# One-hots of low index digits moved from VectorE to ScalarE, and a node piece's first products one slot later, in a two-layer graph network on one core

## What is computed

```python
summed = jax.ops.segment_sum(h[src], dst, num_segments=N_NODES)
return h @ W_self + (summed * deg_inv[:, None]) @ W_neigh + b
...
h = relu(sage_conv(x, ...W_self1, W_neigh1, b1))
h = sage_conv(h, ...W_self2, W_neigh2, b2)
x = layernorm(x + h)
```

## Time and profile before

| | us |
|---|---|
| median of 3 runs | 8132.46 |
| lowest and highest | 8115.67, 8134.15 |
| profiled execution | 8146.79 |
| its span | 8144.9 |

### The profile page before, as it was taken

The page is one execution under the profiler, slowest core; times in us unless marked ns, Lnnn a source line. Parts: engine busy times, 40 slices in busy tenths (PEclk is TensorE's granted clock), DMA queues, the critical chain, the costliest instruction groups (busy, mean ns, idle before and its releaser), DMA issues. The chain is left out here.

```text
span 8144.9 us, 106831 instructions
## 1 busy us (share of the span) xinstructions
PE 6048.0 (74%) x32520; PEld 3961.2 (49%) x32520; DVE 5361.4 (66%) x11308; ACT 2438.4 (30%) x2998; POOL 5785.3 (71%) x5857
## 2 busy tenths in 40 slices
PE   5678787777766788888767777777777777777776
PEld 4555555444444556555534444444444444444444
DVE  8988877676754555555366666666666666666666
ACT  2111111111111000000034444444444444444454
POOL 7777665555555777777757777777777777777776
PEclk8889988888887998899878888888888888888888
DMA  4466667666666898898744444444444444444443
GB/s 123 150 196 234 222 229 246 223 234 221 235 235 228 289 313 302 303 309 305 258 151 130 130 131 131 129 133 131 129 132 133 132 134 134 133 133 132 134 135 103
DMA packets 598851, 1523.91 MB, mean 187 GB/s; under 512 B 157137, under 2 KB 290917, under 8 KB 587014
## 3 DMA queue, kind: packets, MB, share of 16 engines
q1 hardware_dynamic: 411075, 1133.17, 41.0%
q0 software_dynamic: 187200, 383.76, 16.6%
HBM read 1374.92 MB, written 141.47 MB: 186 GB/s over the span
## 5 line engine op out<-in xcount | busy, mean ns | idle before, releaser
L1704 POOL DMA_INDIRECT messages_rows<-y_d,src_idx x3125 | 3043.2, 974 | 1003.3 <-issue 949.0
L1110 POOL DMA_INDIRECT sum_x_rows<-in_x,sum_x_edges x1525 | 1572.5, 1031 | 848.0 <-issue 427.9
L1110 POOL DMA_INDIRECT sum_z_rows<-z_d,sum_z_edges x1200 | 1168.1, 973 | 478.7 <-issue 347.6
L1782 PE MATMUL messages_p_msg<-Wm_e,messages_gated 128*128 128x128 f32 x6250 | 1002.8, 326 | 496.4 <-DVE messages_below L1907 496.1
L1782 PEld LDWEIGHTS messages_p_msg<-Wm_e,messages_gated 128*128 128x128 f32 x6250 | 926.5, 235 | 876.2 <-issue 875.1
L1897 DVE TENSOR_TENSOR messages_p_msg<-messages_p_msg,messages_rows 128x1024 f32<-128x1024 f32 x391 | 481.6, 1232 | 1207.8 <-DMA messages_rows<-y_d,src_idx 1024.8
L1212 PE MATMUL sum_x_build<-sum_x_key_hot,sum_x_low_hot 128*128 128x490 bf16 (+2 forms) x2900 | 833.5, 374 | 230.0 <-DVE sum_x_counts L1408 225.4
L1814 ACT ACTIVATE messages_parts<-messages_p_msg 128x1024 bf16<-128x1024 f32 x391 | 400.1, 1023 | 1808.7 <-DVE messages_p_msg L1897 1808.7
L1232 PE MATMUL sum_z_p_loaded<-sum_z_split,sum_z_counts 128*128 128x384 bf16 x2744 | 794.3, 347 | 160.7 <-DMA sum_z_split<-z_parts_d 156.7
L1408 DVE SCALAR_TENSOR_TENSOR sum_x_counts<-sum_x_counts,sum_x_build 128x980 f32 (+3 forms) x635 | 647.6, 1020 | 356.9 <-PE sum_x_build L1212 346.1
L1232 PE MATMUL sum_x_p_prod<-sum_x_split,sum_x_counts 128*128 128x385 bf16 x2744 | 692.2, 345 | 190.8 <-DMA sum_x_split<-x_parts_d 163.6
(11 more groups left out here) (273 smaller groups left out, 9173.7 us busy)
## 6 DMA issues: line engine op xcount, KB each, us to landing
sum_x_split<-x_parts_d SPq DMA_DIRECT2D x392, 675.5 KB
sum_z_split<-z_parts_d SPq DMA_DIRECT2D x392, 675.5 KB
messages_when<-in_edge_weight SPq DMA_DIRECT2D x391, 512.0 KB, 4.0
messages_attr<-in_span_attr SPq DMA_DIRECT2D x391, 256.0 KB
counts_d<-sum_x_counts SPq DMA_DIRECT2D x28, 3136.0 KB
sum_z_counts<-counts_d SPq DMA_DIRECT2D x56, 1568.0 KB
messages_rows<-y_d,src_idx POOLq DMA_INDIRECT x3125
sum_x_rows<-in_x,sum_x_edges POOLq DMA_INDIRECT x1525
```

The lines of the kernel that those rows point to most:

```text
L1110: nc.gpsimd.indirect_dma_start(out=rows[:, s % depth, j, :], out_offset=None, in_=table, in_offset=bass.IndirectOffsetOnAxis(ap=edges[:, b ...
L1704: nc.gpsimd.indirect_dma_start(out=rows[:, g % SPAN_DEPTH, j, :], out_offset=None, in_=d["y"], in_offset=bass.IndirectOffsetOnAxis(ap=src_ ...
L1782: last = nc.tensor.matmul(p_msg[:, j * P:(j + 1) * P], gated[:, g % SPAN_GATEDS, j * P:(j + 1) * P], t.Wm_e[:], start=True, stop=True)
```

## The change

The low-digit one-hot of five counted tiles is made on ScalarE, in both sums, by six instructions in place of VectorE's one: five Abs of 128 columns (the digit as the bias, so that each gives the distance of the column to the digit) into a new buffer `low_far`, and one Relu of 1 minus that over 640 columns into `low_hot`. ScalarE does it in the slot in which VectorE did, after the copy of the group's one-hot and before everything else. It waits for the digits (`keys_ready`), for the ring (`built`) and for its own instructions. VectorE's `keys_of` now waits until ScalarE has read the digits of two chunks ago. In sum_x, step 3 of a piece on TensorE becomes step 4, and step 4 on ScalarE step 5.

```diff
     def tensor(pe, n, s):
-        if s == 3:
+        if s == 4:
             pe.wait_ge(xT_in, n * 16 + 16)
...
     def scalar(act, n, s):
-        if s == 4:
+        if s == 5:
             act.wait_ge(hB_set, 2 if fast else 1)
...
     low_hot = sb("low_hot", [P, lows, P], BF16)
+    low_far = sb("low_far", [P, TILES, P], BF16)
...
+    low_far_ready = sem("low_far_ready")
...
-                    if first and n == 0 and step == 3:
+                    if first and n == 0 and step == 4:
                         begin.tensor_pieces(pe)
...
+            def low_tiles(u):
+                chunk, at = u // BODY, u % BODY
+                act.wait_ge(keys_ready, chunk * KEY_LINKS + 5)
+                wait_for(act, built, plan.unit_of[u - lows + TILES - 1] + 1 if u >= lows else 0)
+                wait_for(act, low_hot_ready, u // TILES)
+                for j in range(TILES):
+                    last = nc.scalar.activation(low_far[:, j, :], t.iota[:], ACT.Abs, bias=low[:, chunk % 2, at + j:at + j + 1], scale=-1.0)
+                last.then_inc(low_far_ready, 1)
+                act.wait_ge(low_far_ready, u // TILES + 1)
+                nc.scalar.activation(low_hot[:, u % lows:u % lows + TILES, :], low_far[:], ACT.Relu, bias=t.ones_col[:, 0:1], scale=-1.0
+                                     ).then_inc(low_hot_ready, 1)
...
                     nc.scalar.copy(hot16[:, s % WINDOW_HOTS], hot[:, s % WINDOW_HOTS]).then_inc(hot_halved, 1)
+                for u in tiles_of(units_at[s]):
+                    if u % TILES == 0:
+                        low_tiles(u)
                 for b, z in clears_at[s]:
...
                 dve.wait_ge(counted_in[chunk % 3], 16 * (chunk // 3 + 1))
+                wait_for(dve, low_hot_ready, (chunk - 1) * UNROLL)
...
-                if u % TILES == 0:
-                    wait_for(dve, built, plan.unit_of[u - lows + TILES - 1] + 1 if u >= lows else 0)
-                    nc.vector.tensor_tensor(
-                        low_hot[:, u % lows:u % lows + TILES, :], t.iota[:].unsqueeze(1).to_broadcast([P, TILES, P]),
-                        low[:, ring, at:at + TILES].unsqueeze(2).to_broadcast([P, TILES, P]), ALU.is_equal).then_inc(low_hot_ready, 1)
```

## The result

The changed kernel took 8083.75 us (median of 4 runs, 8075.42 to 8090.3) against 8129.35 us (8115.67 to 8134.15). The ratio is 0.9942, with an interval of 0.9925 to 0.9959: 0.58% or 47 us faster, where 100 us were forecast. The profiled execution took 8090.3 us, 56.5 us less than that of before.

The account below looks back on a forecast made before the run. It took sum_z as paced by GpSimd, and sum_x after 600 us as TensorE and VectorE waiting in turn. Terms -40 - 85 - 10 - 45 + 45 + 15 + 20 gave -100 us: 8032, 8-in-10 range 7860 to 8165.

Parts of the forecast that it names:

- Until 600 us: -40: Early sum_x: relieving VectorE gains 40 us (bounds 0 and 53), limited by GpSimd's lead.
- Products one slot later, -85 and clock -10: Sum_x pieces: the `z_rest` wait goes, partly filled by building a unit, -85 us; products at a higher clock, -10.
- Counts, -45: Sum_x after 600 us: TensorE's 92.5 us of waits for VectorE's counts shrink, -45 us (bounds 0 and -92).
- Flips, +45: 28 slots where a block's product ends: new ScalarE instructions ahead of the clears delay the copies, +45 us.
- Late one-hots, +15: Where a chunk of 25 tiles begins: ScalarE's one-hot comes 1.6 us later than VectorE's did, +15 us in all.
- Table chunks, +20: Sum_x: a faster TensorE asks for table chunks sooner and waits longer for them, +20 us (0 to +65).
- Sum_z, 0: Sum_z: GpSimd's gathers set the pace, so the change is worth between 0 and -57 us, taken as 0.
- The price of a group: ScalarE's five Abs and one Relu for five tiles: 2.4 us, with bounds 2.0 and 2.8.
- GpSimd's pace: Rival in sum_x: removed waits free both engines until GpSimd sets the pace; -250 us, 7882, chance 0.16.
- waits renamed: Rival: TensorE's waits only change name, about 8125, chance 0.12; its sign is GpSimd's wait hardly moving.
- slower through ScalarE's order: Rival at the 28 flips: a block pays 5 to 8 us, not 2.4; about 8183, chance 0.11.
- The table load at each change of function: Rival on ScalarE: Abs and Relu share no table and reload at 1.283 us; about +120, 8250, chance 0.03.

Follow-up runs that it names:

- flips_first: The changed kernel with ScalarE's low one-hots behind the clears and copies in slots that copy a product; ratio 0.9869 to the kernel before.
- tables_first: The changed kernel with ScalarE's low one-hots behind the clears and table split, still ahead of the product copies; ratio 0.9895 to the kernel before.
- one_hots_last: The changed kernel with ScalarE's order in every slot: table split, product copies, clears, low one-hots, piece steps; 7969.17 us, ratio 0.9793 to the kernel before.
- pieces_only: The kernel before with only the pieces' products one slot later, low one-hots left on VectorE; ratio 0.9909, 74 us faster.
- digits_only: The changed kernel with the piece steps put back, low one-hots still on ScalarE; ratio 1.0025 to the kernel before, 20 us slower.
- order_without_digits: The kernel before with products one slot later and product copies ahead of clears, low one-hots on VectorE; ratio 0.9878 to the kernel before.
- the two repairs: The changed kernel with early_on_vector and flips_first joined; 7995.49 us, ratio 0.9828 to the kernel before.
- early_on_vector: The changed kernel with the low one-hots of sum_x's first 300 tiles (slots 10 to 40) left on VectorE; ratio 0.9916 to the kernel before.
- copies_first: The changed kernel with early_on_vector and flips_first joined, and the clears also behind the product copies; ratio 0.9801 to the kernel before.

## Why the prediction was wrong

**The sign and the later terms held; the early path did not.** The failed step is the first term, *Until 600 us: -40*. It reckoned with VectorE, relieved, and GpSimd, at its pace, and with nothing else: ScalarE's order was priced at the flips and where chunks begin, but never in the early slots, where it holds the table split that VectorE waits for. In its place stood a loop through both engines: at slot 84, near 600 us, the kernel was 13 us late, and not 40 us early. (About 12 us of this gap are the first flips, which the forecast had in another term: flips_first reaches slot 84 at 595.2 us.) From there to the end of sum_x it gained 55 us (13 us late, then 42 early), where the forecast's later terms add up to -60. So this one step is most of the miss. With the split copies ahead (tables_first) the kernel is 38 us faster than the changed one and 29 us early at slot 84; in one_hots_last it is 39 us early. That this is just the 40 of the forecast is in part luck: GpSimd's lead at that place was 25 us, not up to 53, and shorter gathers, which the forecast did not have, gave the other 18.

**Products one slot later, -85 and clock -10.** Right in kind: alone they gave 74 us for 95. Two sizes were off against each other. The fill by a unit was overrated, as 40 of the 113 us that left `z_rest` became waits for counts; the clock was underrated: the products took 37 us less, where 30 were reckoned, and the flips took hardly any of it back (55.4 us busy before, 56.4 after), where 20 were taken off.

**Counts, -45.** The wait itself reads 92.5 and 95.9, as if the term were nothing. Taken from pieces_only it is 36 us (132.1 to 95.9): about right, and covered by what the pieces had renamed. Together with the early term, -85 for VectorE's relief stands beside the 69 us that the digits brought when they stood last, late one-hots included.

**Flips, +45.** Right: the wait grew by 51 us, and putting the one-hots behind the copies took that away and brought 60. **Late one-hots, +15**: after 600 us only 5.8 us; the 69.6 us before that were mostly the loop's. **Table chunks, +20**: +11. **Sum_z, 0**: its gathers changed little, as 63.4 for 56.8 us of waits for TensorE show; sum_z itself took 7 us less.

**The price of a group** was estimated at 2.4 us with Abs 0.38 and Relu 0.79; it measured 0.386, 0.828 and 2.34 to 2.5. By the rule of the Trainium skill (ScalarE: Activation LUTs, section Rules for kernel authors) this work belongs on VectorE. Its factor of up to about 3 is for bf16 instructions with one source; here six instructions on ScalarE (2.5 us) stand against one on VectorE with two fp32 sources (0.82 us), so that the ratio is near 3 does not test it. Digits_only is slower, as the rule would have it, but one_hots_last and order_without_digits differ by 69 us the other way: price alone did not decide here, and the place in ScalarE's list did.

**The rivals.** GpSimd's pace did not take over in this kernel: from 600 us on its wait for TensorE stayed at 410 us, and one_hots_last brought it to 289. (Until 600 us TensorE waits for gathers in one_hots_last, 34.2 us for 3.3 before.) The prediction named an unmoved wait as its sign of waits renamed; it misled. Over all of sum_x the gathers themselves took 70 us less (1572.5 and 1502.7 us busy), more than the stage became shorter, so GpSimd's wait had to grow, and did, from 418.8 to 444.0 us. Waits did change their name, in part (40 us to counts in pieces_only). The case slower through ScalarE's order had the right engine and the wrong place: 60 us at the flips, and some 40 more at the split, which it didn't name. With the digits alone it came true, by 20 us. The table load at each change of function is out: sum_x still has one load, of 1283 ns. This agrees with the Trainium skill (ScalarE: Activation LUTs, section Table sets: the hidden batching unit), by which cheap functions such as relu, copy and abs are in every set.

**What stays open.** That the two repairs together give more (93 us) than singly (21 and 60) lies inside the intervals. So does the difference of tables_first (38) and early_on_vector (21) in time. At slot 84 they are 13 us apart (564.6 and 577.1); that this is VectorE's relief in the early slots, which only tables_first keeps, was not tested by itself. The orders were tried in this one program, and the 25 us of the clears and the 22 of copies_first are hardly clear of the intervals.

## What to carry to other kernels

An engine that idles most of a stage still runs a list in order: before work is moved onto it, write down every instruction that comes to stand behind the new one, in each phase of the stage, and who waits for that. Here the work was needed a slot later and belonged behind the hand-offs of its slot: the same instructions cost 27 us in front (on top of the pieces) and gave 69 us at the end (on top of the same order without them). A wait that does not change between two profiles may be two changes that cancel: one part alone shows them.

## What the hardware showed beside this

GpSimd's gathers in sum_x became shorter when VectorE lost the low one-hots (count | busy us, mean ns; pieces_only, where VectorE keeps them, then the changed kernel):

```profile
L1110 POOL DMA_INDIRECT sum_x_rows<-in_x,sum_x_edges x1525 | 1564.8, 1026 | 772.5 <-issue 434.0 <-PE sum_x_win L1200 337.3 <-DMA sum_x_edges<-in_edges 1.3
```

```profile
L1112 POOL DMA_INDIRECT sum_x_rows<-in_x,sum_x_edges x1525 | 1502.7, 985 | 873.2 <-PE sum_x_win L1202 444.0 <-issue 427.7 <-DMA sum_x_edges<-in_edges 1.2
```

The kernel before has 1031 ns and order_without_digits 1029; digits_only has 987 and one_hots_last 995. That is 50 to 70 us of GpSimd's time in sum_x, which the prediction did not have. The Trainium skill (GPSIMD Engine Reference, section 1, Specifications) says that GpSimd shares its SBUF interfaces with VectorE and contends with VectorE instructions with two SBUF inputs; the removed one-hot is such an instruction. The trace of the kernel before agrees on such instructions, sorted by what VectorE was running when a gather began:

| VectorE at the start of a gather | gathers | mean ns |
|---|---|---|
| nothing | 281 | 945 |
| counting a unit (L1408, one input in SBUF, one in PSUM) | 326 | 947 |
| a key one-hot (L1394, one input in SBUF, and a scalar) | 352 | 1052 |
| a group's one-hot (L976, both inputs in SBUF) | 89 | 1126 |
| a low one-hot (L1388, both inputs in SBUF) | 170 | 1252 |
| subtracting a split part (L1412, both inputs in SBUF) | 28 | 1437 |

So it is the gathers beside instructions with two SBUF inputs that last longest. Those beside a key one-hot last longer too, which the number of inputs does not explain, and no run changed the place of an input alone: the mechanism itself is not shown.
